# A mixture-of-experts layer on one core: routed rows kept as two 16-bit halves, and the experts' second matrix in an array and a transfer of its own

## What is computed

```python
scores = sigmoid(x @ gate_w)                       # 2048 x 32
# the 2 best of 4 groups of 8 experts, in them the 6 best experts
weights = weights / sum(weights)
g = ragged_dot(xs, w_gate, group_sizes)            # rows sorted by expert
u = ragged_dot(xs, w_up, group_sizes)
d = ragged_dot(silu(g) * u, w_down, group_sizes)
expert_out = sum(out * weights[..., None], axis=1)
shared = silu(x @ sw_gate) * (x @ sw_up) @ sw_down
return expert_out + shared
```

## Time and profile before

| what | us |
|---|---|
| median of three runs | 1949.65 |
| the profiled execution | 1951.45 |
| its span, first to last instruction | 1949.6 |
| attention and what is ahead of it | to about 1403 |
| token tiles, choice, shared expert, scatter | about 1403 to 1565 |
| routed tiles | about 1565 to 1899 |
| combine | to 1949.6 |

### The profile page before, as it was taken

How to read it: one execution, slowest core, us unless ns; L and a number is a source line. 1 busy time by engine, 2 the same in 40 slices (tenths; PEclk the granted TensorE clock), 3 DMA queues, 4 the chain that set the end, 5 groups by cost and what they waited for, 6 DMA issues and landing times. The chain is left out here.

```text
span 1949.6 us, 43870 instructions
## 1 busy us (share of the span) xinstructions
PE 1851.4 (95%) x13730; PEld 981.7 (50%) x13730; DVE 1254.6 (64%) x2826; ACT 1384.7 (71%) x1908; POOL 1383.7 (71%) x837
## 2 busy tenths in 40 slices
PE   8979999999999999999999999999889689999986
PEld 6734444444444444444444444444376467777765
DVE  5777777767776777677767776776076345555553
ACT  5617888888888888888888888888752145555543
POOL 1526888988898889888988898889747723333330
PEclk9969999999999999999999999999999889999998
DMA  6100122112111211121112211000024379999979
GB/s 251 49 10 1 65 98 89 66 63 112 74 66 63 110 76 66 63 110 76 66 63 108 78 66 52 8 6 10 7 86 184 135 247 345 338 350 354 346 270 302
DMA packets 104645, 240.00 MB, mean 123 GB/s; under 512 B 24656, under 2 KB 57680, under 8 KB 104464
## 3 DMA queue, kind: packets, MB, share of 16 engines
q1 hardware_dynamic: 93840, 209.18, 30.2%
q0 software_dynamic: 10752, 30.16, 4.0%
HBM read 130.66 MB, written 104.37 MB: 121 GB/s over the span
## 5 line engine op out<-in xcount | busy, mean ns | idle before, releaser
L899 POOL TENSOR_TENSOR prob_lo<-prob,prob_hi 128x1024 f16<-128x1024 f32 x512 | 1080.8, 2129 | 166.4 <-ACT prob_hi L928 166.4
L974 DVE TENSOR_REDUCE maxes<-ring 128x1 f32<-128x512 f32 x1024 | 645.2, 684 | 232.4 <-PE ring L1065 229.9
L926 ACT ACTIVATE prob<-p_s,prob_scale 128x1024 f32<-128x1024 f32 x512 | 571.1, 1115 | 212.2 <-PE p_s L1084 190.7
L928 ACT ACTIVATE prob_hi<-p_s,prob_scale 128x1024 f16<-128x1024 f32 x512 | 570.3, 1114 | 0.0
L1065 PE MATMUL ring<-kr_hi,qr_hi 64*128 64x512 f16 x1024 | 374.8, 384 | 7.7 <-DVE qc_hi L961 4.2
L1065 PE MATMUL ring<-kc_pair,qc_hi 64*128 64x512 f16 x1024 | 371.3, 383 | 0.0
L1084 PE MATMUL p_s<-qr_lo,kr_hi 64*128 64x512 f16 x1024 | 287.0, 375 | 0.0
L1084 PE MATMUL p_s<-qr_hi,kr_lo 64*128 64x512 f16 x1024 | 286.5, 376 | 0.0
L1353 POOL DMA_INDIRECT ranked_out<-y,dest x128 | 123.1, 962 | 216.2 <-DVE y L1660 213.5
L1084 PE MATMUL p_s<-qr_hi,kr_hi 64*128 64x512 f16 x1024 | 244.2, 380 | 1.6 <-ACT prob_hi L928 1.6
L1084 PE MATMUL p_s<-qc_lo,kc_one 33*128 33x512 f16 x1024 | 242.4, 378 | 0.0
(11 more groups left out here) (248 smaller groups left out, 2447.4 us busy)
## 6 DMA issues: line engine op xcount, KB each, us to landing
w<-in_experts SPq DMA_DIRECT2D x128, 608.0 KB, 5.3
expert_rows<-zeros SPq DMA_DIRECT2D x129, 544.0 KB, 4.7
rows<-expert_rows SPq DMA_DIRECT2D x128, 136.0 KB, 4.7
got<-ranked_out SPq DMA_DIRECT2D x16, 768.0 KB, 10.4
wqb<-in_wqb SPq DMA_DIRECT2D x8, 768.0 KB, 4.9
recip_wide<-prob_recips SPq DMA_DIRECT2D x64, 64.0 KB
cbar<-att_t SPq DMA_DIRECT2D x64, 64.0 KB, 2.0
cbar<-in_woT SPq DMA_DIRECT2D x1, 2048.0 KB, 16.8
```

The lines of the kernel that those rows point to most:

```text
L899: gp.tensor_tensor(prob_lo[s % NB][:, :], prob[s % 2][:, :], prob_hi[s % NB][:, :], ALU.subtract).then_inc(lo_ready, 1)
L926: act.activation(prob[s % 2][:, :], p_s[s % 2][:, :], ACT.Exp, bias=prob_scale[:, :], scale=SCALE / W_SCALE)
L928: act.activation(prob_hi[s % NB][:, :], p_s[s % 2][:, :], ACT.Exp, bias=prob_scale[:, :], scale=SCALE / W_SCALE).then_inc(p_ready, 1)
L974: best = v.tensor_reduce(maxes[:, at:at + 1], bank[:, :], AX.X, ALU.max)
```

## The change

In the token tiles the normalized row goes into one of four new tiles, normed, from which turn_h reads it. A new function, split_row, writes into hall, in the bytes of the same 256 f32 columns, 256 f16 values (the row, cast) and 256 more (the row less its cast). It stands one iteration behind normalize in VectorE's loop and ahead of that iteration's pieces of the choice. turn_rows turns the halves as f16 products with an f16 unit matrix: for each of the two blocks of 128 columns two products that add up in PSUM. The array experts becomes experts_in (34 x 128 x 704) and experts_out (34 x 88 x 512), and each load of weights becomes two transfers, in the loop, ahead of it and for the shared expert; TensorE and POOL wait for twice the count.

```diff
--- before.py
+++ after.py
@@ -1179,6 +1179,8 @@
         eps = sb("eps2", 1)
         mcol = sb("mcol", 2 * DK)
         hall = sb("hall", T * RW)
+        normed = [sb(f"normed{n}", D) for n in range(4)]
+        ident16 = sb("ident16", P, F16)
         h2T = sb("h2T", T * D)
         sc = sb("sc", T * E)
         tmp = sb("tmp", T * E)
@@ -1290,14 +1292,17 @@
             sp.wait_ge(moved, MOVES * last + 64)
             spread_recips(sp, last, scaling, moved)
             for n in range(2):
-                sp.dma_start(ws[n][:, :], a["experts"][E + n, :, :]).then_inc(ld_ws, 16)
+                sp.dma_start(ws[n][:, 0:WIN], a["experts_in"][E + n, :, :]).then_inc(ld_ws, 16)
+                sp.dma_start(ws[n][0:MH, WIN:WIN + WOUT], a["experts_out"][E + n, :, :]).then_inc(ld_ws, 16)
             sp.wait_ge(answered, 2 * last + 2)
             store_heads(sp, last, scaling, cbar, stored)
 
             def load_weights(i, u):
                 e = sp.value_load(tile_expert[0:1, ds(i + u, 1)], min_val=0, max_val=E - 1)
                 sp.wait_ge(y_mm, i + u + 1)
-                sp.dma_start(w[u][:, :], a["experts"][ds(e, 1), :, :].rearrange("a p n -> (a p) n")).then_inc(w_ld[u], 16)
+                sp.dma_start(w[u][:, 0:WIN], a["experts_in"][ds(e, 1), :, :].rearrange("a p n -> (a p) n")).then_inc(w_ld[u], 16)
+                sp.dma_start(w[u][0:MH, WIN:WIN + WOUT],
+                             a["experts_out"][ds(e, 1), :, :].rearrange("a p n -> (a p) n")).then_inc(w_ld[u], 16)
 
             def load_rows(i, u, first=False):
                 r = sp.value_load(tile_row[0:1, ds(i + u, 1)], min_val=0, max_val=E * S)
@@ -1331,7 +1336,7 @@
             gp.wait_ge(pads, 1)
             gp.tensor_copy(t3(hall, RW)[:, :, D], tokens[:, :]).then_inc(pads, 1)
             gp.wait_ge(pads, 2)
-            gp.wait_ge(ld_ws, 32)
+            gp.wait_ge(ld_ws, 64)
             for n in range(2):
                 down = ws[n][0:MH, WIN:WIN + WOUT].rearrange("p (k d) -> p k d", k=2)
                 gate_b = mod[0:MH, 5 * D:6 * D].rearrange("p (k d) -> p k d", k=1).to_broadcast([MH, 2, D])
@@ -1454,8 +1459,18 @@
                 v.wait_ge(root_ready, t + 1)
                 v.wait_ge(var_ready, t + 1)
                 step(v.reciprocal(rstd[:, t:t + 1], rstd[:, t:t + 1]))
-                v.tensor_scalar(hall[:, t * RW:t * RW + D], xt, mv[:, t * 2:t * 2 + 1], rstd[:, t:t + 1],
+                if t >= len(normed):
+                    v.wait_ge(t_mm, t - len(normed) + 1)
+                v.tensor_scalar(normed[t % len(normed)][:, :], xt, mv[:, t * 2:t * 2 + 1], rstd[:, t:t + 1],
                                 ALU.subtract, ALU.mult).then_inc(h_ready, 1)
+
+            def split_row(t):
+
+                pair = hall[:, t * RW:t * RW + D].bitcast(F16)
+                full = normed[t % len(normed)]
+                v.wait_ge(h_ready, t + 1)
+                step(v.tensor_copy(pair[:, 0:D], full[:, :]))
+                v.tensor_tensor(pair[:, D:2 * D], full[:, :], pair[:, 0:D], ALU.subtract)
 
             def invert():
 
@@ -1585,16 +1600,19 @@
                 step(v.tensor_tensor(pick[:, :], pick[:, :], wn[:, :], ALU.mult))
                 step(v.tensor_reduce(t3(weight, 8)[:, :, j], t3(pick), AX.X, ALU.add))
 
+            step(v.tensor_copy(ident16[:, :], ident[:, :]))
             v.wait_ge(col_mm, 1)
             v.tensor_copy(mcol[:, :], p_y[0][:, :].rearrange("p (n c) -> p n c", n=4)[:, :, 0]).then_inc(col_ready, 1)
             v.wait_ge(pads, 1)
             pieces = {"scores": scores, "best_groups": best_groups, "inside_groups": inside_groups, "best_experts": best_experts,
                       "count": count_group, "place": place}
-            for t in range(T + 1):
+            for t in range(T + 2):
                 if t < T:
                     token_tile(t)
-                if t >= 1:
+                if 1 <= t <= T:
                     normalize(t - 1)
+                if t >= 2:
+                    split_row(t - 2)
                 if t == 2:
                     invert()
                 if t == 4:
@@ -1696,7 +1714,7 @@
                 if t >= 2:
                     pe.wait_ge(t_ready, t - 1)
                 for k in range(DK):
-                    last = pe.transpose(p_t[t % 2][:, k * P:(k + 1) * P], hall[:, t * RW + k * P:t * RW + (k + 1) * P],
+                    last = pe.transpose(p_t[t % 2][:, k * P:(k + 1) * P], normed[t % len(normed)][:, k * P:(k + 1) * P],
                                         ident[:, :])
                 last.then_inc(t_mm, 1)
 
@@ -1782,7 +1800,7 @@
                                      stop=(n % 2 == 1 and k == 1))
                 last.then_inc(sd_mm, 1)
 
-            pe.wait_ge(ld_ws, 32)
+            pe.wait_ge(ld_ws, 64)
             pe.wait_ge(folded, 2)
             for n in range(2):
                 shared_gate(n)
@@ -1802,13 +1820,17 @@
             def turn_rows(n, u, ring):
                 pe.wait_ge(row_ld[u % U], ring)
                 pe.wait_ge(r_used, n + 1)
+                pair = rows[u % U][:, 0:D].bitcast(F16)
                 for k in range(DK):
-                    last = pe.transpose(p_r[u % 2][:, k * P:(k + 1) * P], rows[u % U][:, k * P:(k + 1) * P], ident[:, :])
+                    for half in range(2):
+                        at = half * D + k * P
+                        last = pe.matmul(p_r[u % 2][:, k * P:(k + 1) * P], pair[:, at:at + P], ident16[:, :],
+                                         start=(half == 0), stop=(half == 1))
                 last.then_inc(r_mm, 1)
 
             def gate_up(n, u, ring):
                 pe.wait_ge(r_used, n + 3)
-                pe.wait_ge(w_ld[u % U], ring)
+                pe.wait_ge(w_ld[u % U], 2 * ring)
                 pe.wait_ge(hid_ready, n + 1)
                 for k in range(DK):
                     last = pe.matmul(p_g[u % 2][:, 0:2 * M], rT[u % 2][:, k * P:(k + 1) * P],
@@ -1964,8 +1986,7 @@
 
     w_in = np.concatenate([w_in, shared_in]).reshape(E + 2, DK, P, 2 * M).transpose(0, 2, 1, 3).reshape(E + 2, P, WIN)
     w_down = np.concatenate([given["L0_ffn_w_down"], sw_down.reshape(2, M, D)])
-    w_out = np.zeros((E + 2, P, WOUT), f32)
-    w_out[:, :MH] = w_down.reshape(E + 2, 2, MH, D).transpose(0, 2, 1, 3).reshape(E + 2, MH, WOUT)
+    w_out = w_down.reshape(E + 2, 2, MH, D).transpose(0, 2, 1, 3).reshape(E + 2, MH, WOUT)
     arrays = {
         "x": given["L0_attn_x"].reshape(S, D),
         "c": given["L0_c"].reshape(DK, P).T,
@@ -1981,7 +2002,8 @@
         "cos": np.concatenate([cos, cos]).reshape(ROPE, 2, 2, QC).transpose(2, 0, 1, 3).reshape(P, 2 * QC),
         "sin": np.concatenate([sin, -sin]).reshape(ROPE, 2, 2, QC).transpose(2, 0, 1, 3).reshape(P, 2 * QC),
         "gate": given["L0_ffn_gate_w"],
-        "experts": np.concatenate([w_in, w_out], axis=2),
+        "experts_in": w_in,
+        "experts_out": w_out,
         "lower": np.triu(np.ones((P, P), f32), 1),
         "own": np.arange(SLOT_TILES * P, dtype=f32).reshape(SLOT_TILES, P).T,
         "tokens": (SLOT_TILES * P + np.arange(S, dtype=f32)).reshape(T, P).T,
```

## The result

| | median, us | lowest to highest | runs |
|---|---|---|---|
| before | 1951.24 | 1948.52 to 1953.75 | 4 |
| after | 2045.88 | 2043.01 to 2047.85 | 4 |

The ratio is 1.050, with a 95% interval of 1.048 to 1.052: slower, as forecast, but by 95 us instead of 68, and above the range's upper end of 2036. The profiled execution took 2046.61 us, its span 2044.8.

The account below looks back on a forecast made before the run. The prediction took SP's own issue sequence in the routed tiles, 2.58 us a tile, as the bound. It summed 1951.45 + 6.9 + 63 - 1 = 2020, or 2018 us against the median, range 1997 to 2036.

Parts of the forecast that it names:

- SP sets the pace: Routed-tile loop: SP's own instruction sequence, 2.58 us a tile against the array's 2.49, sets the period; it becomes 3.11.
- Rival 1: Routed tiles: bytes and the array are the bound, an extra issue costs SP nothing that counts; 1949 us, chance 6%.
- The loop's term, +63: SP's loop: one more weights transfer issued per tile, 0.53 us each, 120 times; +63 us (46 to 74).
- rival 2: Routed tiles: DMA engines set the pace, 88 rows spread over eleven of them, 0.05 us a tile; 1963 us, chance 4%.
- The scatter's delay, +6.9: Token tiles: thirteen VectorE splits ahead of the second place() delay POOL's scatters through to the end; +6.9 us (4 to 12).
- The products, 0: Routed tiles: four f16 products replace two f32 transposes on the array, hidden by SP; cost 0, uncovered 0 to 26 us.
- The landing, -1: End of the routed tiles: fewer weight bytes let the last rows land sooner; -1 us (0 to -2).
- Rival 3: Routed tiles: the array's idling makes its clock fall throughout, a tile needs twice 2.49 us; 2245 us, chance 3%.

## Why the prediction was right in kind and wrong in size

**SP sets the pace: right.** The step grew to 3.30, with no wait in it but the first, rows landed sooner, and the array idles 15.7 us in 100 and 31 tiles, 0.5 a tile, put down to rows. The idle register load shows the same with no transfer added. Rival 1 falls with it (bytes and the array as the bound): it would have needed SP's step under 2.49. The Trainium skill's sentence in "DMA: Bandwidth & Descriptors", section "Issuing engines are not separate DMA queues", compares the time to initiate a DMA with the DMA itself and calls it usually small. As a ratio this agrees with the trace, 0.34 us for an issue against 3.0 us from there to the landing of the rows, so the prediction's "the trace disagrees" reads too much into it. What the trace shows is that a small issue can stand on the path all the same: 0.53 us with its register work, in a step of 3.30.

**The loop's term, +63: the step that failed.** Its own price was right: 120 x 0.531 = 64 us for the three instructions of L1304, against 120 x 0.53. What failed is "it is the same instruction", taken to the end that only its own duration counts. The register load behind it grew by 0.226 us, 27 us over 120 tiles, and 4 us came back at tile_expert's load: 87 instead of 63, and past the 74 of the upper end. These are 24 of the 28 us between 2018 and 2046. No row of the kernel before shows a transfer of 88 rows, as the prediction says itself at rival 2, and yet the term priced it by one of 128. With 96 rows the term would have held: step +0.485, 58 us; with 128 too: +0.551, 66 us.

**The scatter's delay, +6.9: right, partly by luck.** 7.5 measured. The two instructions of the split take 0.285 and 0.426, near the 0.30 and 0.43 of the forecast. First L1472, then L1473, then what POOL waited for:

```profile
L1472 DVE CAST hall<-normed x16: 274/285/288, 1414.3 to 1464.5; 128x256 f16<-128x256 f32 x16
```

```profile
L1473 DVE TENSOR_TENSOR hall<-normed,hall x16: 424/426/438, 1414.7 to 1464.8; 128x256 f16<-128x256 f32 x16
```

```profile
POOL expert_rows L1349 <- DVE slot L1557: 18.4, 2, 11.4
```

The wait for the second group's slots grew from 6.1 to 11.4, and POOL's first scatter starts 2.6 us later (1433.9 against 1431.3), so the second group's scatters begin 7.9 us later (1460.33 against 1452.47). Thirteen splits are 9.8 us with the gap; of these the forecast let 3.1 vanish in VectorE's waits for the array, but by the traces these waits shrank by 1.0 only (7.9 to 6.9). And one pair of executions measures this term only roughly: in the six traces with the halves the first rows are issued between 1566.4 and 1570.1, in the six without between 1560.9 and 1566.4, on average 6.2 us apart.

**Not in the sum: +2.1 at the start.** The array began the routed tiles at the lower clock in both kernels, but stayed there longer after. Its timeline, before and after, from the first group of gate and up products to the first down products:

```profile
1566.51 2.72 PE L1814 MATMUL bank<-w,rT 128*128 128x352 f32 x4 [0.90 <-ACT rT L1363]
...
1570.55 1.45 PE L1814 MATMUL bank<-w,rT 128*128 128x352 f32 x4 [0.90 <-ACT rT L1363]
...
1574.40 1.03 PE L1829 MATMUL bank<-w,hidT 88*128 88x256 f32 x4
```

```profile
1573.92 2.72 PE L1836 MATMUL bank<-w,rT 128*128 128x352 f32 x4 [0.90 <-ACT rT L1368]
...
1577.96 2.72 PE L1836 MATMUL bank<-w,rT 128*128 128x352 f32 x4 [0.90 <-ACT rT L1368]
...
1584.03 1.03 PE L1851 MATMUL bank<-w,hidT 88*128 88x256 f32 x4
```

The first group takes 2.72 us in both, at 1.2 GHz. The second takes 1.45 before, at 2.4 GHz, and still 2.72 after, and the first down product comes 9.6 us later, not 7.4 like the first two groups. SP's only wait grew with it, 4.0 to 6.1. This is not the change's doing for the most part: from the first rows to the loop's first weights it is 13.0 us in the trace of the kernel before, but 14.4 with the idle load and 14.6 with one register load a tile, where the array's work up to there is the same, and 15.1 after. The one profiled execution of before was early; when the clock comes back varies between executions.

**The products, 0: right, with its cover.** SP hides the array's 2.55 us. Without that cover the 0.06 behind the f16 group would count, some 7 us over 120 tiles, inside the 0 to 26 named.

**The landing, -1: right in number, not shown to come of the bytes.** -1.1 from the last rows to the end. But the version with the padded transfer, which saves no byte, has 64.5 us there and lands its rows after 3.4; with the idle load it is 66.2 and 4.1. So the fewer bytes are not needed for it, and from one execution each a us or two stays open.

**Rival 2 (DMA engines unevenly loaded): not the bound here, but its spreading is real.** The transfers of 88 rows bring 11 small packets each, so they run on eleven engines. The Trainium skill, "DMA: Bandwidth & Descriptors", section "Why a DMA increments its semaphore by 16 and not by 1", has the rule that gives eleven for 88 rows, and says that the issuing sequencer itself writes the increments of the engines left out. The traces agree with both: the twelfth update, 0.49 us after the issue starts, is such a write. All four traces with 88 rows have this update and the slow load; the four that split off 96 or 128 rows have neither. Whether the write is what slows the load is not shown. In the kernel after it falls into the load, which starts 0.45 us behind the issue. But with the issue moved, and with one load a tile, the slow load starts only about 1.0 us behind the issue, half a microsecond after the update. Rival 2's own claim, that the engines set the pace, needs SP relieved, and even then SP's own sequence held nearly the whole step.

**Rival 3 (the clock falls throughout):** no. From 1585 to 1980 the granted clock averages 0.99, with some 16 us in 100 idle. It did leave 1.00, which the prediction had named as a sign of being wrong, but only for two stretches of 3.4 us.

## What to carry to other kernels

When a queue's own sequence sets the period, price a new instruction on it by its duration and by what it does to the instructions behind it, register loads too. Try a shape of transfer in the regime in which it will run. While SP set the pace, only the 88 rows cost more than the issue itself, through the register load, and 96 rows were no worse than 128. With SP relieved, 96 rows cost 8 us over the kernel before and 128 rows none: there the zeros were cheaper than leaving them out. And look at the sequence itself first: one register load less a tile gave 5 us, where no version with fewer bytes gained anything.

## What the runs showed of the hardware that was not expected

- A register load on SP takes 272 ns, and 446 as the next one behind the issue of a transfer of 88 rows, even with another issue between them. Behind 96 or 128 rows it stays at 270.
- A transfer of 88 rows brings 11 packets of 4 B, one of 96 or 128 rows 16, one for each engine as far as the runs tell, and with 88 rows one semaphore update comes 0.49 us after the issue starts, ahead of all data.
- Beside a transfer of 128 rows, one of 96 fills the DMA engines at 317 GB/s and lands in 9 us, its packets taking 104 ns at the median instead of 84; one of 128 carries 359 GB/s with it and lands in 4.6.
- A value read from a table into a register costs SP 0.56 us of its step (2.58 to 3.14), as much as a whole transfer's issue (0.52 to 0.53).
- The first of a group of f32 products behind four f16 products of 128 columns takes 515 ns instead of 462.
